# Top-two choice split across a stage's beginning, and sums moved from VectorE to GpSimd and ScalarE, in a 12-layer transformer kernel

## The reference, cut to what matters

```
def _L2_ffn_ref(x, w_gate, w_in, w_out):          # E = 8 experts, TOP_K = 2
    xt = x.reshape(-1, D)
    logits = (xt @ w_gate.T).astype(jnp.float32)
    top_logits, top_idx = jax.lax.top_k(logits, TOP_K)
    top_gates = jax.nn.softmax(top_logits, axis=-1).astype(x.dtype)
    gates = (jax.nn.one_hot(top_idx, E, dtype=x.dtype) * top_gates[..., None]).sum(axis=1)
    y = jnp.zeros_like(xt)
    for e in range(E):
        h = xt @ w_in[e].T
        y = y + gates[:, e:e + 1] * (h @ w_out[e].T)
    return y.reshape(B, S, D)
...
x = x + 0.5 * _L1_ffn_ref(_layernorm(x), ...)
x = x + 0.5 * _L2_ffn_ref(_layernorm(x), ...)
x = x + _L2_attn_ref(_layernorm(x), ...)          # a recurrence over time
x = x + 0.5 * _L2_ffn_ref(_layernorm(x), ...)
x = x + 0.5 * _L3_ffn_ref(_layernorm(x), ...)     # tokens are scattered to their experts
```

## Time and profile before

| what | us |
|---|---|
| median of 3 runs | 1414.59 (1413.01 to 1416.67) |
| profiled execution, its own time | 1414.04 |
| its span, first to last instruction | 1412.3 |
| ffn2_0 in that span | 808.8 to 856.9 |
| rec2 | 856.9 to 884.3 |
| ffn2_1 | 884.3 to 949.0 |

### The profile page before, as it was taken

How to read it: one execution, slowest core, us unless ns; L and a number is a source line. 1 busy time by engine, 2 the same in 40 slices (tenths; PEclk the granted TensorE clock), 3 DMA queues, 4 the chain that set the end, 5 groups by cost and what they waited for, 6 DMA issues and landing times. The chain is left out here.

```text
span 1412.3 us, 30262 instructions
## 1 busy us (share of the span) xinstructions
PE 1173.9 (83%) x11551; PEld 686.9 (49%) x11561; DVE 869.1 (62%) x2263; ACT 649.0 (46%) x1346; POOL 585.5 (41%) x727
## 2 busy tenths in 40 slices
PE   3895889886968979999969886846985999898698
PEld 3582444444845645566536534333771233233377
DVE  5146778842155678788535598871177889893205
ACT  1222566651432446766632252421453777685143
POOL 5763244113541669987310112163743033123352
PEclk9997799997968989999989896867995799999699
DMA  7542333105710186666229000013433122110344
GB/s 138 154 113 79 94 105 98 45 11 141 223 41 1 38 231 193 181 190 200 78 39 112 8 2 1 3 46 109 132 95 101 47 80 80 34 37 17 87 143 119
DMA packets 137674, 128.66 MB, mean 91 GB/s; under 512 B 19245, under 2 KB 120377, under 8 KB 137536
## 3 DMA queue, kind: packets, MB, share of 16 engines
q1 hardware_dynamic: 127392, 103.46, 28.0%
q0 software_dynamic: 10080, 23.31, 5.0%
q10 hardware_dynamic: 64, 0.04, 0.0%
HBM read 79.80 MB, written 47.69 MB: 90 GB/s over the span
## 5 line engine op out<-in xcount | busy, mean ns | idle before, releaser
L2803 DVE TENSOR_REDUCE att_maxima<-psum 128x2 f32<-128x1024 f32 (+3 forms) x384 | 353.4, 950 | 78.2 <-PE psum L2496 32.7
L2695 ACT ACTIVATE att_probs<-psum 128x512 f32<-128x512 f32 (+1 forms) x640 | 323.6, 555 | 155.6 <-PE psum L2466 55.0
L124 POOL TENSOR_TENSOR rstd<-var_eps,neg_half 128x2 f32<-128x2 f32 x88 | 61.6, 704 | 335.9 <-DVE var_eps L97 332.4
L2449 PE MATMUL psum<-att_queries,att_keys 50*32 50x384 bf16 (+4 forms) x1280 | 159.2, 330 | 23.3 <-ACT att_probs L2695 11.3
L2455 PE MATMUL psum<-att_keys,att_queries 48*32 48x384 bf16 (+4 forms) x1280 | 157.5, 345 | 12.4 <-DVE att_maxima L2803 12.1
L1144 POOL DMA_INDIRECT returned<-moe_out,moe_slot_tokens x101 | 100.9, 999 | 108.7 <-DVE moe_out L1068 79.3
L926 ACT ACTIVATE moe_hidden<-psum,moe_b 128x320 f32<-128x320 f32 (+1 forms) x128 | 77.7, 607 | 112.2 <-PE psum L833 111.7
L2449 PEld LDWEIGHTS psum<-att_queries,att_keys 50*32 50x32 bf16 (+1 forms) x1280 | 46.2, 92 | 144.2 <-issue 69.8
L833 PE MATMUL psum<-moe_slot_columns,moe_w 128*128 128x320 f32 (+1 forms) x256 | 99.9, 535 | 3.1 <-ACT moe_slot_columns L921 2.9
L644 POOL DMA_INDIRECT dispatched<-normalised_rows,route_scatter_i x64 | 63.8, 998 | 80.7 <-DVE route_scatter_i L624 51.4
L840 PE MATMUL psum<-moe_w,moe_hidden 128*128 128x128 f32 x784 | 93.5, 277 | 0.0
(11 more groups left out here) (303 smaller groups left out, 2347.6 us busy)
## 6 DMA issues: line engine op xcount, KB each, us to landing
moe_w<-l_w SPq DMA_DIRECT2D x64, 256.0 KB, 3.1
score_terms<-att_parts SPq DMA_DIRECT2D x32, 384.0 KB, 2.7
moe_back<-returned SPq DMA_DIRECT2D x24, 256.0 KB, 4.2
att_queries<-score_terms SPq DMA_DIRECT2D x64, 96.0 KB
att_keys<-score_terms SPq DMA_DIRECT2D x64, 96.0 KB
att_queries<-score_terms SPq DMA_DIRECT2D x16, 384.0 KB, 4.2
att_keys<-score_terms SPq DMA_DIRECT2D x16, 384.0 KB, 5.5
score_terms<-att_parts POOLq DMA_DIRECT2D x12, 384.0 KB, 3.2
```

The costliest lines, as they stand in the source:

```text
L2449: col = nc.tensor.matmul(g.psum[one, cols_bank + h, c0:c0 + w], k_op[own_rows, ci, p, key], q_op[own_rows, ci, p, first_query[s]:T], start ...
L2695: nc.scalar.activation(probs[:, G % 2, 2 * p + r, unit_at[u]:unit_at[u] + w], g.psum[:, cols_bank + r, 0:w], ACT.Exp).then_inc(probs_ready, 1)
L2803: ins = nc.vector.tensor_reduce(maxima[:, G % 2, t, 2 * p:2 * p + 2], g.psum[:, rows_bank(k):rows_bank(k) + 2, c0:c0 + w], axis=AX, op=ALU ...
```

## The change

- **The choice in two parts.** A new class `TopTwo` chooses and weighs for a range of tiles. For ffn2_0 the tiles 0 to 7 are chosen and weighed in the last batch of ffn1_1 (`split` = 2 batches), the tiles 8 to 15 in ffn2_0 itself, during batch 1. For ffn2_1 the tiles 0 to 11 (`split` = 3) are chosen and weighed at the end of rec2, the tiles 12 to 15 in ffn2_1 during batch 1.
- **The last batch's rows move.** ffn1_1 no longer makes root, rows, columns and logits of batch 3; ffn2_0 does (`closing`).
- **Sums on GpSimd.** The two halving additions go to GpSimd for batches 0 to 2 in ffn2_0 and 0 to 1 in ffn2_1.
- **Rows on ScalarE.** Batches 0 to 2 get their normalised rows from ScalarE (`scalar_rows`, L164); VectorE makes one small product for them (`shifts`, L152). Batch 3 stays on VectorE.
- In rec2 the logits of batch 2 come before the turn of batch 3, on TensorE and on ScalarE.

```
+class TopTwo:
+    def choose(self, v, half, c):
...
+        for step in range(5):
+            self.after(v, first_max_step(g, step, scores[:, at, :], self.best[:, c, at], self.work[:, at, :],
+                                         self.onehot[:, c, at, :], self.tie[:, at]))
...
+    def exponential(self, act, half):
+        at = self.tiles(half)
+        act.wait_ge(self.exp_in, half + 1)
+        self.g.nc.scalar.activation(self.delta[:, at], self.delta[:, at], ACT.Exp).then_inc(self.exp_out, 1)
+    def weigh(self, v, half):
...
+        ops.tensor_tensor(self.weight[:, at, :], self.work[:, at, :], self.others[:, at, :], ALU.add).then_inc(self.weighted, 1)
...
 def ffn1 ... @block.vector
+                if top and b == B - 1 and c in (2, 3):
+                    v.wait_ge(ln.logits, top.split)
+                    top.choose(v, 0, c - 2)
+                if top and (b, c) == (B - 1, chunks - 1):
+                    top.weigh(v, 0)
...
 def ffn2 ... @block.vector
             for b in range(B):
+                if b == top.split:
+                    v.wait_ge(top.weighted, 2)
                 add_pair(b, 0)
+                if closing and b == 0:
+                    ln_rows(g, v, closing, B - 1)
+                if b == 1:
+                    if closing:
+                        v.wait_ge(closing.logits, B)
+                    for c in range(2):
+                        top.choose(v, 1, c)
                 if b >= 1:
                     add_shares(b - 1)
...
                 add_pair(b, 1)
+                if b == 1:
+                    top.weigh(v, 1)
...
                 if b >= 1:
-                    ln_rows(g, v, ln, b - 1)
+                    norm.shifts(v, b - 1)
...
         @block.gpsimd
+            def sum_shares(b):
+                pool.wait_ge(scaled, GROUP * GROUP * (b + 1))
+                nc.gpsimd.tensor_tensor(share(b, 0, 2), share(b, 0, 2), share(b, 2, 4), ALU.add).then_inc(pool_halved, 1)
+                pool.wait_ge(pool_halved, b + 1)
+                nc.gpsimd.tensor_tensor(share(b, 0, 1), share(b, 0, 1), share(b, 1, 2), ALU.add).then_inc(pool_summed, 1)
...
+            sum_shares(0)
             for b in range(B):
                 ln_rstd(g, pool, ln, b)
+                if b + 1 in by_pool:
+                    sum_shares(b + 1)
```

More of the change, by code:

```diff
@@ L1472, in _ @@
                 begun.zero_values(pool)
-            for b in range(B):
+            for b in range(B - 1 if top else B):
                 if begun and b == 2:
@@ L1525, in ffn2 @@
+def ffn2(g, name, products, top, gate=None, prefetch=None, routing=None, begun=None, closing=None):
     nc, a = g.nc, g.a
@@ L1545, in ffn2 @@
         routed = B - 1 if routing else 0
+        by_pool = range(2 if routing else 3)
+        norm = SharedNorm(g, sb, ln, 0)
+        share = lambda b, lo, hi: shares[:, b % 2, lo:hi, :, :]
         def read(b, u):
@@ L1580, in _ @@
                 at = k % len(order)
+                if closing and (b, at) == (0, 5):
+                    ln_transpose(g, pe, closing, B - 1, rank_bank)
+                if closing and (b, at) == (0, 7):
+                    ln_logits(g, pe, closing, B - 1, rank_bank)
                 if at == 3 and b >= 2:
@@ L1632, in _ @@
                 scale(b, 3)
+                if closing and b == 0:
+                    ln_copy_logits(g, act, closing, B - 1, rank_bank)
+                if b == 1:
+                    top.exponential(act, 1)
+                if b >= 1:
+                    norm.scalar_rows(act, b - 1)
             for b in range(B - 2, B):
@@ L1854, in _ @@
             turn(2)
+            logits(2)
             turn(3)
-            logits(2)
             logits(3)
@@ L1905, in _ @@
             ln_rows(g, v, ln, 3)
+            v.wait_ge(ln.logits, top.split)
+            for c in range(2):
+                top.choose(v, 0, c)
+            top.weigh(v, 0)
         @block.gpsimd
```

141 lines of the change are left out of this document (88 added, 53 removed).

## The result

The changed kernel takes 1416.51 us (median of 20 runs, 1408.89 to 1423.92) against 1410.96 for the kernel before (20 runs beside them, 1403.04 to 1416.67): a ratio of 1.0039, 95% interval 1.0025 to 1.0054. That is 5.5 us slower, 3.5 to 7.6; the forecast was 3.7.

A forecast was written before the change was run, and what follows sets the result against it. VectorE was taken to bound ffn2_0 and the scatters to end ffn2_1; -1.3 and +5.0 make +3.7 on 1414.04, 1417.7, and 0.55 for the median gives 1418.3 us. Own range 1416 to 1420.5, wider range 1410.8 to 1422.

The forecast's parts named there:

- The sign that would have failed it: In ffn2_1, the first scatter moving by less than 4 us against the stage before would fail the forecast.
- Start of ffn2_0: Choosing early in ffn1_1's last batch lets ffn2_0 start at 805.4 instead of 808.85: -3.4 us.
- Batch 0 and the first pair of batch 1: In ffn2_0, slow TensorE units pace VectorE: second pair at 815.4 (was 818.9), batch 1's first at 820.0 (was 822.3).
- The sum on GpSimd: Two halving additions on GpSimd take 2.0 and 1.16 us, 3.2 a batch, against 1.9 on VectorE.
- The rival of slow sums: Sums on GpSimd take 3.9 us a batch, deciding from 3.4, in both stages: +7.2, 1421.8; chance 0.23.
- What VectorE loses beside GpSimd: In ffn2_0, VectorE steps with SBUF inputs are held until GpSimd's instruction ends: +3.3 us, bounds 0 and 4.5.
- the scan came out at -1.0 for -1.3: End of ffn2_0: -4.6 unhindered plus 3.3 of holding makes -1.3 us.
- End of rec2: Later last copy, table load, exponential and weighing form a chain ahead of ffn2_1, which starts later: +3.8 us.
- ffn2_1 to the first scatter: Lost ready units, second choice and holding delay ffn2_1's first scatter by +5.8 us, +2.0 counted from its first unit.
- From there on: In ffn2_1, first to last scatters: -0.8 us, second group 13.0 to 13.3 behind the first, third 14.2 later.
- The rival without holding: Short VectorE steps slip between GpSimd's: ffn2_0 -4.6, ffn2_1 +2.8, in all -1.8, 1412.8; chance 0.17.
- The faster start: TensorE's clock returns 1 us sooner at ffn2_0 and ffn2_1, nothing is held: -4.3, 1410.3; chance 0.10.

The follow-up runs named there:

- e10: Changed kernel with the late choice in ffn2_1, plus dummy matmuls keeping TensorE at work ahead of and within ffn2_0; -8.8 us against the kernel before.
- e6: Changed kernel plus eight dummy matmuls on TensorE behind rec2's last logits, ahead of ffn2_1; +3.7 us against the kernel before.
- e1: Changed kernel with the two halving additions of all batches back on VectorE; +8.0 us against the kernel before.
- e4: Changed kernel, but GpSimd starts each next batch's sum only after VectorE's shift of the batch ahead; +4.9 us against the kernel before.
- e9: e7 with GpSimd's sums also waiting for VectorE's weighing (batch 1) and the previous batch's shift; +1.6 us against the kernel before.
- e7: Changed kernel plus dummy matmuls on TensorE in mid-stage of ffn2_0 and ffn2_1, ten before batch 2, six before the first turn; +1.4 us against before.
- e5: Changed kernel with an extra unread exponential on ScalarE in rec2, so the table load comes earlier; +1.9 us against the kernel before.
- e11: Kernel before with only the rows moved to ScalarE; choice late in both stages, all sums on VectorE; -6.1 us against the kernel before.

## Why the prediction was right, step by step, and where it was not

The time and the direction are within the forecast's own range: slower, by 5.5 where 3.7 was said. The forecast was worked from 1414.59, the median of three runs; over 20 runs the kernel before has 1410.96, so 1418.3 is 1.8 above the time, while the difference is 1.8 too small. That it is no more is in part luck: the pieces of the traces add up to +7.1, four of the six errors went the same way, and the time happens to show less of them. By the forecast's own yardstick of 4.2 us, the 5.5 (3.5 to 7.6) count rather as slower, to which it gave 0.35, than as no change, to which it gave 0.55. The sign that would have failed it did not come: counted from ffn2_0's scan, the first scatter moved by 7.8.

- **Start of ffn2_0**: -3.9 for -3.4. Right.
- **Batch 0 and the first pair of batch 1**: the second pair of tiles ended at 820.28, the first pair of batch 1 at 825.04; less the 5.15 by which this profile is late, 815.1 and 819.9, forecast 815.4 and 820.0. Right, with its reason: the choice had covered TensorE's slow start. The clock in ffn2_0, start and mid-stage together, is worth 2.3 us in e10; the start of ffn2_1 alone 2.7 in e6.
- **The sum on GpSimd**: mis-sized. 2.35 and 1.27 for 2.0 and 1.16, so 3.7 a batch for 3.2. The rival of slow sums put its turning point at 3.4 and its total at +7.2, near the traces' +7.1. But e1 shows that its mechanism isn't the loss: with the sums taken off GpSimd the first scatter came 1.7 sooner, ffn2_0 took 1.5 more, and the kernel is no faster.
- **What VectorE loses beside GpSimd**: all the places are there, and larger: weighing +1.9 (said 0.9), shift +2.0 (1.6), the two additions +0.9 each (1.0 each). The Trainium skill (SBUF — State Buffer, Who interferes with whom) says that an fp32 `tensor_scalar` may take the shared ports too. L1587's 1.14 us over 8 columns agrees, and it was the half of the weighing's 1.9 that my sum left out. As a term to be added up in ffn2_0, though, the step failed: e4 and e9 both remove 1.9 and 2.0 of it, and get 0.2 and nothing there. That the scan came out at -1.0 for -1.3 is therefore in part luck: length of sum and holding are mostly the same microseconds, and holding was added as a cost of its own. In ffn2_1 holding did cost something, by way of ScalarE's rows (see below).
- **End of rec2**: +3.8 for +3.8 (+3.0 to +3.2 in the traces of e4, e7 and e9, whose code is the same there), with 1.4 of it the table load (e5). The Trainium skill (ScalarE: Activation LUTs, What ACT_TABLE_LOAD costs) adds a drain of 1.38 to a load. Here the exponential starts at 890.15, 1.29 after the load's start, and moving the load away gave 1.4, not 2.7: no drain, as the earlier trace rows had it.
- **ffn2_1 to the first scatter**: +4.0 for +2.0, the largest error. VectorE was ready for the routing 29.0 us after the stage's start, where before it was 27.0: +2.0, where the sum had +1.4. There it waited 2.03 for the first logits, where the sum had 0.6: this is the term that was mis-sized. Two things made the wait, and the sum has neither as a delay of the logits. The held weighing makes `shift` 1.8 late, and ScalarE's rows, the turn and the logits with it (e4). And TensorE, starved behind the second choice, falls to 0.50 a second time, so that `shift` to logits takes 6.4 us and not 4.9 as in e7 at full clock. Without the one the wait is gone (e4), without the other it is 0.52 (e7). The prediction asked what the choice uncovers at the start, and not what it does to TensorE where it was put.
- **From there on**: the second group 12.83 behind the first, just outside the 13.0 to 13.3 said, the third 14.58 for 14.2. The last piece, +0.9, is mostly the landing of the second scatters of batch 2 (GpSimd waits 4.28 for it, before 3.62); the piece varies between 20.0 and 21.1 in the runs.

The rival without holding is excluded by the rows. The faster start, whose condition is TensorE's clock, had the right mechanism with nothing in the change to bring it about; e10 brings it about.

What stays open: the 4 to 5 us by which e10 and e11 are faster than their four stages explain (e7: 3.6), and whether the sums on GpSimd earn anything beside rows on ScalarE. Single traces can't settle the first: up to batch 2's rows in ffn1_1 e9's profiled execution took 797.97 us and e10's 792.76, with the same code there and on the same chip.

## What to carry to other kernels

Work that looks like a bare delay at a stage's start may be what lets another engine fill its banks; taken away, it shows that engine's own slow start, and put into the middle it can starve it there. Ask for each moved block which engine is starved by it at the new place, and whether that engine slows down when idle. And a step that is held beside another engine's long instruction isn't simply a cost to add to that instruction's length. Where the holding engine's result is waited for anyway, both can be the same wait (ffn2_0). It counts where a third engine's work hangs on the held step (ScalarE's rows in ffn2_1). So follow both, and take the one that ends last.
